# Rank counts of a token routing as two fp32r matmuls instead of three f32 matmuls

## What is computed

```python
raw = jnp.einsum('bsd,ed->bse', x, centroids)
balanced = jax.nn.sigmoid(raw + routing_bias)
_, top_idx = jax.lax.top_k(balanced, TOP_K)
gathered = jnp.take_along_axis(routing_scores, top_idx, axis=-1)
top_w = jax.nn.softmax(gathered, axis=-1)
h_sh = jax.nn.gelu(jnp.einsum('bsd,nfd->bsnf', x, Wfc_sh), approximate=False)
h_r = jax.nn.gelu(jnp.einsum('bsd,efd->bsef', x, Wfc_r), approximate=False)
```

## Time and profile before

| | before |
|---|---|
| time, median of 3 runs (lowest to highest) | 253.06 us (252.71 to 253.97) |
| the profiled execution: its own time | 252.87 us |
| its span, first to last instruction | 251.1 us |
| TensorE: matmul busy, share | 242.7 us, 97% |
| VectorE busy | 153.5 us, 61% |
| ScalarE busy | 135.5 us, 54% |
| GpSimd busy | 50.2 us, 20% |
| mean granted TensorE clock | 0.998 |
| matmul records | 1908 |

### The profile page before, as it was taken

The page is one execution under the profiler, slowest core; times in us unless marked ns, Lnnn a source line. Parts: engine busy times, 40 slices in busy tenths (PEclk is TensorE's granted clock), DMA queues, the critical chain, the costliest instruction groups (busy, mean ns, idle before and its releaser), DMA issues.

```text
span 251.1 us, 5120 instructions
## 1 busy us (share of the span) xinstructions
PE 242.7 (97%) x1908; PEld 209.4 (83%) x1908; DVE 153.5 (61%) x371; ACT 135.5 (54%) x265; POOL 50.2 (20%) x81
## 2 busy tenths in 40 slices
PE   8799998999999999999999999999999999999994
PEld 8656645366367599999998999999999999999994
DVE  0833244453654897788849246666667666667683
ACT  2225205152152778886867256666666666666641
POOL 5100000000100200230587002112122111126700
PEclk9999999999999999999999999999999999999999
DMA  7999999999999999950157448999999999920142
GB/s 253 423 432 397 423 407 431 377 404 425 356 379 341 323 315 426 422 238 0 45 169 295 105 130 287 364 373 364 360 354 349 371 346 360 347 117 21 54 137 84
DMA packets 14254, 74.12 MB, mean 295 GB/s; under 512 B 1524, under 2 KB 8956, under 8 KB 9884
## 3 DMA queue, kind: packets, MB, share of 16 engines
q1 hardware_dynamic: 12700, 70.59, 74.9%
q0 software_dynamic: 1008, 2.76, 2.9%
q10 hardware_dynamic: 528, 0.52, 0.6%
HBM read 67.56 MB, written 6.32 MB: 294 GB/s over the span
## 4 chain that ended last, share of the span: by engine, by line
PE 71%; DMA 15%; DVE 4%; POOL 3%; issue 2%; SPq 2%; ACT 2%; DVEq 0%; POOLq 0%; ACTq 0%
PE psum L512 61%; DMA rows<-rows_dram 11%; PE psum L760 4%; POOL slot_x_dram L479 3%; DMA slot_x_dram<-second,rows_of 3%; PE psum L601 2%; PE psum L778 1%; DMA xrow<-slot_x_dram 1%; ACT prob L879 1%; DVE cmax L1083 1%; PE psum L821 1%; SPq L337 1%; PE psum L650 1%; PE psum L692 0%; DVE xs L1107 0%
## 5 line engine op out<-in xcount | busy, mean ns | idle before, releaser
L512 PE MATMUL psum<-xrowT,ring 128*128 128x128 f32 x480 | 58.3, 275 | 0.0
L512 PEld LDWEIGHTS psum<-xrowT,ring 128*128 128x128 f32 x480 | 56.2, 192 | 0.0
L1303 DVE TENSOR_TENSOR dlo<-ring,dhi 128x1024 fp32r<-128x1024 f32 x30 | 38.3, 1280 | 3.8 <-ACT dhi L962 3.8
L1322 DVE TENSOR_TENSOR slot_hlo<-slot_h,slot_hhi 128x512 fp32r<-128x512 f32 x30 | 20.8, 693 | 30.0 <-ACT slot_hhi L990 30.0
L988 ACT ACTIVATE slot_h<-psum 128x512 f32<-128x512 f32 x30 | 18.0, 600 | 35.5 <-PE psum L512 35.5
L512 PE MATMUL psum<-dhi,slot_hhi 128*128 128x256 f32 x120 | 36.3, 302 | 0.1
L512 PE MATMUL psum<-dhi,slot_hlo 128*128 128x256 f32 x120 | 33.8, 282 | 0.0
L512 PE MATMUL psum<-dlo,slot_hhi 128*128 128x256 f32 x120 | 33.8, 282 | 0.0
L962 ACT ACTIVATE dhi<-ring 128x1024 fp32r<-128x1024 f32 x30 | 31.1, 1040 | 0.0
L504 POOL DMA_INDIRECT results_dram<-y_rows,result_row x13 | 14.6, 1119 | 72.6 <-DMA results_dram<-y_rows,result_row 56.2
L512 PE MATMUL psum<-xh,parted 128*128 128x256 f32 x128 | 26.8, 286 | 0.0
(11 more groups left out here) (195 smaller groups left out, 398.4 us busy)
## 6 DMA issues: line engine op xcount, KB each, us to landing
ring<-experts_dram SPq DMA_DIRECT2D x15, 2048.0 KB, 8.5
ctx<-ctx_dram SPq DMA_DIRECT2D x4, 3072.0 KB, 24.5
ctxT_start<-ctxT_start_dram SPq DMA_DIRECT2D x4, 2048.0 KB, 19.0
ctxT_rest<-ctxT_rest_dram SPq DMA_DIRECT2D x4, 1154.0 KB, 21.4
raw<-experts_dram SPq DMA_DIRECT2D x2, 2048.0 KB, 15.4
slot_x_dram<-empty_row SPq DMA_DIRECT2D x1, 1935.0 KB, 16.2
xrow<-slot_x_dram SPq DMA_DIRECT2D x15, 129.0 KB, 7.4
squares<-squares_dram SPq DMA_DIRECT2D x1, 1285.0 KB, 14.2
```

Of the source, the lines that this page charges most:

```text
L512: return pe.matmul(out, lhsT, rhs, start=first, stop=last)
L1303: dve.tensor_tensor(dlo[b % 2][:, steps, :], ring[b][:, steps, C * P:STEP_W], dhi[b % 2][:, steps, :].bitcast(F32), ALU.subtract).then_inc ...
L1322: dve.tensor_tensor(slot_hlo[:, half, :], slot_h[:, half, :], slot_hhi[:, half, :].bitcast(F32), ALU.subtract).then_inc(slot_hlo_ready, 1)
```

## The change

The three f32 matmuls of `ranks` become two with fp32r operands (32-bit numbers that TensorE multiplies with rounded mantissas). All values are whole numbers: `tri` and `ones_r` hold 0 and 1, `chosen` 0 and 1, `before` at most 4. `before` gets a fifth row, which takes the place of `total`, so one product of 40 columns gives the earlier tiles' sums and the counts. `tri`, `chosen` and `before` become fp32r, there is a new constant `ones_r`, and POOL fills fp32r tensors by a copy instead of a memset.

```diff
-        tri = sb("tri", [P, P])
+        tri = sb("tri", [P, P], F32R)
+        ones_r = sb("ones_r", [P, P], F32R)
         ones = sb("ones", [P, P])
...
-        chosen = sb("chosen", [P, T, ROUTED])
-        before = sb("before", [P, T, ROUTED])
-        total = sb("total", [P, ROUTED])
+        chosen = sb("chosen", [P, T, ROUTED], F32R)
+        before = sb("before", [P, T + 1, ROUTED], F32R)
...
-            link(pool.memset(tri[:, :], 1.0))
-            pool.affine_select(out=tri[:, :], in_=tri[:, :], compare_op=ALU.is_ge, fill=0.0, base=-1,
+            pool.tensor_copy(ones_r[:, :], ones[:, :])
+            pool.affine_select(out=tri[:, :], in_=ones[:, :], compare_op=ALU.is_ge, fill=0.0, base=-1,
                                pattern=[[1, P]], channel_multiplier=-1).then_inc(consts, 1)
...
-            link(pool.memset(before[:, 0, :], 0.0))
+            link(pool.tensor_copy(before[:, 0, :], empty_row[:, 0:ROUTED]))
...
                 pe.wait_ge(chosen_ready, 1)
+                mm(bank(RANK_BANK, 0, (T + 1) * ROUTED), ones_r[:, :], before[:, :, :].rearrange("p t e -> p (t e)"),
+                   True, False)
                 mm(bank(RANK_BANK, 0, T * ROUTED), tri[:, :], chosen[:, :, :].rearrange("p t e -> p (t e)"),
-                   True, False)
-                mm(bank(RANK_BANK, 0, T * ROUTED), ones[:, :], before[:, :, :].rearrange("p t e -> p (t e)"),
-                   False, True)
-                mm(bank(RANK_BANK, T * ROUTED, ROUTED), ones[:, :], total[:, :], True, True).then_inc(rank_ps, 1)
+                   False, True).then_inc(rank_ps, 1)
...
                 link(dve.tensor_tensor(chosen[:, :, :], hot[:, 0, :, :], hot[:, 1, :, :], ALU.add))
-                for t in range(1, T):
-                    link(dve.tensor_tensor(before[:, t, :], before[:, t - 1, :], chosen[:, t - 1, :], ALU.add))
-                dve.tensor_tensor(total[:, :], before[:, T - 1, :], chosen[:, T - 1, :], ALU.add
-                                  ).then_inc(chosen_ready, 1)
+                for t in range(1, T + 1):
+                    ins = dve.tensor_tensor(before[:, t, :], before[:, t - 1, :].bitcast(F32),
+                                            chosen[:, t - 1, :].bitcast(F32), ALU.add)
+                    if t < T:
+                        link(ins)
+                ins.then_inc(chosen_ready, 1)
```

## The result

The change takes 252.45 us (median of 22 runs, 251.57 to 253.41); the kernel before, measured beside it, 252.94 us. The ratio is 0.9974, with a 95% interval of 0.9964 to 0.9984: 0.66 us less, between 0.40 and 0.91. By the medians it is 0.49 us. One of the 22 runs of before took 851.46 us, for a reason that nothing here shows; the others took 252.35 to 253.97, and the medians hardly feel it. The forecast was 0.32 us less. The sign is right, the size too small, and the experiments show which term was missed.

A forecast was written before the change was run, and what follows sets the result against it. Two nearly level paths were taken to bound the kernel: TensorE's own work and the later route through VectorE, POOL and DMA. That route's gain gave 253.06 - 0.32 = 252.7 us, range 252.1 to 253.6.

The forecast's parts named there:

- The price of a pass, 0.11 us: TensorE's rank counts: each matmul pass costs 0.11 us whatever its columns, so six passes cost 0.66 us and two 0.22.
- one pass for an fp32r product: TensorE's rank counts: each fp32r product goes in one pass, where each f32 matmul took two.
- VectorE's limit: VectorE behind the rank counts: `place` gains only 0.15 us; the `hlo` of unit 14 and `rows_of` gain 0.32.
- The slower rival: POOL's eight indirect DMA issues meet a worse phase of VectorE's work, adding up to 2.25 us: 255.0 us, chance 0.05.
- The first slot's rows arrive at 140.23: End of the route through VectorE, POOL and DMA: the first slot's rows land 0.32 us earlier, at 140.23 us.
- the route through POOL is now the later one by 0.33 us: At the first slot's turn on TensorE, the POOL route still decides, by 0.33 us instead of 0.21.
- the landing and the read: The last scatter's landing, 6.72 us, and the first slot's read, 2.93 us; the landing was assumed to keep its length.
- TensorE's own 0.44 us: TensorE's own work up to the first slot's turn: it arrives there 0.44 us earlier, bounds 0.42 and 0.60.
- TensorE's wait at the turn: Before the change, TensorE waits 0.21 us for the first slot's rows when it starts turning them.
- the gain did not stop at the landing: Rival: the last scatter's rows arrive when they did before, so nothing is gained: 253.1 us, chance 0.22.
- the passes were halved and more: Rival on TensorE's rank counts: fp32r with few columns still takes two passes, four remain: 252.8 us, chance 0.08.
- The copies on POOL were covered: POOL at the start: two copies of 0.58 us each cost nothing, since POOL idles 3.03 us for VectorE.

The follow-up runs named there:

- e3: The change with four more fp32r products of 40 columns ahead of the pair, results overwritten, so six passes again; 252.99 us, ratio to before 1.0002.
- e6: The change with 12 instead of 10 warm-up matmuls at the start of TensorE's program, eight instructions more; 252.28 us.
- e12: The change with nine more fp32r passes of 40 columns, result unused, on TensorE ahead of hid 28, when the scatters are issued; 253.59 us.
- e7: The change with the last of the first four ring loads asked for behind the reads of the first slots' rows; 252.41 us, ratio to before 0.9971.
- e9: The kernel before, with only the last ring load asked for behind the reads of the rows; 252.86 us, ratio to before 0.9997.
- e1: The kernel before with the totals folded into a fifth row of `before`, all in f32: two matmuls, four passes; 252.56 us, ratio to before 0.9982.
- e2: The change with the totals as a product of their own: three fp32r products, three passes; 252.54 us, ratio to before 0.9974.
- e11: The change with five more dependent VectorE additions of 128x32, result unused, ahead of place_tokens; 252.61 us.

## Why the prediction was right, and where not

- **The price of a pass, 0.11 us, and one pass for an fp32r product:** right. 0.44 us were forecast for TensorE; the group gave 0.90 - 0.46 = 0.44, and e3 shows that the price is the same for the new kind. The table of isolated gaps in the Trainium skill ("TensorE: Matmul & The Clock Gate", section "Back-to-back issue gap"), by which the passes would be worth 0.10 us, does not hold for passes with a weight load each; the section itself says that at small N it under-counts them. So the skill does not speak against the price as the prediction has it.
- **VectorE's limit:** right. `place` moved by 0.16 (0.15 forecast), the `hlo` of unit 14 by 0.34 (0.32), `rows_of` by 0.35 (0.32).
- **POOL:** the first issue moved by 0.34 and the last by 0.43 (0.32 forecast for both); the eight kept their sum within 0.1 us. The slower rival (issues on a worse phase) did not occur.
- **The step that failed** is the last one, "The first slot's rows arrive at 140.23", and what was built on it, "the route through POOL is now the later one by 0.33 us". It took the landing and the read over from one trace, 6.72 and 2.93 us. The landing did not shorten: it was 7.06 in the change, and 6.4 to 7.1 in all eleven traces with the ring load ahead. The read did: 1.98 us in the change, and 1.9 to 3.6 in the fourteen traces. So the rows came 1.04 us earlier instead of 0.32, ahead of TensorE in both profiles of the change, and TensorE's own 0.44 us counted in full. The wait of before went with it, 0.37 us, so the traces show 0.86 us at the end where I had 0.32. The rank counts are not enough to make the read short, as e6 and e12 show; what made it short in these two traces stays open, and this part of what the traces gained is luck.
- **A wait read too small.** The prediction priced the passes by starts, but took TensorE's wait at the turn from the profile's modelled end: 0.21 us. By starts it is 0.37. The route decided by more than the prediction thought, and still lost its lead with one shorter read.
- **The size.** e7 and e9, where the rows don't matter, put the passes at 0.43 us in their traces; their timed ratios allow 0.2 to 1.2. The change has 0.49 us by medians and 0.40 to 0.91 by the ratio, so the passes can carry most of it. What is left would be the wait for the rows, which e9 puts at 0.08 us in timed runs, at most 0.4. The runs don't settle its share, nor how often it occurs. That the forecast came near is in part luck: the path that it named did not decide, but that path's 0.32 and TensorE's 0.44 are close.
- **The rivals:** the gain did not stop at the landing, and the passes were halved and more. The copies on POOL were covered.

## What to carry to other kernels

Where two paths reach a point within a few tenths of a microsecond, and one ends in DMAs, don't take its length from one trace as a constant: price both cases, and let the steady path give the floor. A small matmul here costs 0.11 us for each pass, with 8, 32 or 40 columns, f32 or fp32r, so count passes, not columns. Measure a wait by starts as well: twice here, at the turn and at the `hlo`, the wait that the profile lists was shorter than the time that was to be won. And once two paths are level, look for the pair of edits that moves both; here each alone gave no clear gain, and together they gave another 0.4%.

## What the runs showed of the hardware that I had not expected

- SP's issue of one of four DMAs took 1.3 to 1.9 us instead of 0.43 in the seven traces where a 16 KB fetch of instructions began beside it: the four together took 3.05 us in the trace of before and 1.76 in the change. The first of the four reads landed after 2.5 to 3.6 us there, and after 1.9 to 2.1 in the other seven.
- Two `dlo` subtractions of 128x1024 beside POOL's additions took 3.14 us in e1 and e2, 4.16 in e11, where the additions began 1.26 us later, and 3.73 to 3.77 in the nine other traces that have the pair there. What sets it was not found. One alone behind the additions took 1.23 us, beside them 2.09.
- The price of 0.11 us a pass held for f32 and fp32r alike, in groups of 2, 3, 4 and 6.
